# First attention one step deeper: a sequence's transposes, values and products behind the next scores, sorting counts a step later

## The reference, cut to what matters

```python
x = x + attn_a(layernorm(x), w_q, w_k, w_v1, w_v2)   # one head, width 64, causal, 512 x 512 scores per sequence
x = x + ffn(layernorm(x), Wg, W1, W2, W3)            # 8 experts, the best 2 of each token
...
queries = einsum('bse,ek->bsk', x, w_q);  keys = einsum('bse,ek->bsk', x, w_k)
attn = softmax(where(causal, queries @ keys.T * scale, -inf))
out = attn @ ((x @ w_v1) @ w_v2)
...
scores = xt @ Wg.T                                   # per token, 8 numbers
topk_scores, topk_idx = top_k(scores, 2)
```

## Time and profile before

| what | us |
|---|---|
| median of 3 runs (lowest, highest) | 1552.91 (1551.44, 1554.37) |
| the profiled execution, its own time | 1549.28 |
| its span, first to last instruction | 1547.5 |
| busy in the span: PE, DVE, ACT, POOL | 1320.2, 1109.0, 951.5, 765.4 |
| `attention_a`, first matmul (67.48) to the experts' first DMA (244.32) | 176.8 |
| start of the scores of steps 0 to 7 | 70.55, 76.81, 84.35, 92.58, 111.26, 129.12, 147.11, 165.04 |
| `slot` of b = 0 to 7 ready (start of line 742 plus 0.21) | 112.93, 130.59, 148.57, 166.50, 185.00, 199.43, 213.93, 227.01 |

### The profile page before, as it was taken

How to read it: one execution, slowest core, us unless ns; L and a number is a source line. 1 busy time by engine, 2 the same in 40 slices (tenths; PEclk the granted TensorE clock), 3 DMA queues, 4 the chain that set the end, 5 groups by cost and what they waited for, 6 DMA issues and landing times. The chain is left out here.

```text
span 1547.5 us, 28434 instructions
## 1 busy us (share of the span) xinstructions
PE 1320.2 (85%) x8377; PEld 1124.9 (73%) x8377; DVE 1109.0 (72%) x2822; ACT 951.5 (61%) x2522; POOL 765.4 (49%) x954
## 2 busy tenths in 40 slices
PE   2687635999759999999999999999999996499990
PEld 1576625888748888888888888888888884388880
DVE  5665444777638788888887888888888874377771
ACT  1554313444338878888788788787888884144440
POOL 3005562444415565576575665765755755244443
PEclk9877657999959999999999999999999996599995
DMA  9391011222100000000000000000000000122215
GB/s 182 122 364 33 30 40 48 57 57 56 31 28 15 1 15 1 1 25 5 3 25 3 17 12 1 22 8 1 11 5 5 11 1 14 39 57 56 56 44 163
DMA packets 91936, 64.47 MB, mean 42 GB/s; under 512 B 34020, under 2 KB 77935, under 8 KB 91792
## 3 DMA queue, kind: packets, MB, share of 16 engines
q1 hardware_dynamic: 83152, 45.75, 11.0%
q0 software_dynamic: 8640, 16.93, 3.5%
HBM read 26.59 MB, written 36.96 MB: 41 GB/s over the span
## 5 line engine op out<-in xcount | busy, mean ns | idle before, releaser
L1360 POOL TENSOR_TENSOR b_probs<-b_probs,b_recip 128x128 f32<-128x128 f32 (+3 forms) x512 | 352.7, 719 | 309.0 <-DVE b_recip L1593 309.0
L420 DVE TENSOR_TENSOR b_pt_lo<-b_ring,b_pt_hi 128x512 fp32r<-128x512 f32 (+1 forms) x384 | 218.9, 598 | 93.1 <-ACT b_pt_hi L414 87.8
L545 ACT ACTIVATE b_probs<-b_s_bank,b_neg_max 128x256 f32<-128x256 f32 (+3 forms) x512 | 267.9, 533 | 27.7 <-DVE b_neg_max L537 26.3
L537 DVE TENSOR_REDUCE b_neg_max<-b_s_bank 128x1 f32<-128x256 f32 (+3 forms) x512 | 219.6, 478 | 49.3 <-PE b_s_bank L529 48.3
L1220 POOL DMA_INDIRECT y_rows<-f_y_sb,f_dest x142 | 139.1, 979 | 215.4 <-DVE f_y_sb L1198 208.1
L414 ACT ACTIVATE b_pt_hi<-b_ring 128x512 fp32r<-128x512 f32 (+1 forms) x384 | 192.3, 547 | 9.1 <-PE b_ring L485 8.4
L81 PE MATMUL b_s_bank<-b_k_hi,b_q_hi 64*128 64x256 f32 (+3 forms) x512 | 181.2, 354 | 2.9 <-ACT b_probs L545 1.4
L485 PE MATMUL b_ring<-ident,b_probs 128*128 128x128 f32 x1280 | 179.4, 278 | 4.7 <-DVE b_q_lo L420 4.7
L82 PE MATMUL b_s_bank<-b_k_lo,b_q_hi 64*128 64x256 f32 (+3 forms) x512 | 164.9, 322 | 0.0
L83 PE MATMUL b_s_bank<-b_k_hi,b_q_lo 64*128 64x256 f32 (+3 forms) x512 | 164.2, 321 | 0.0
L554 PE MATMUL b_pv_bank<-b_pt_hi,b_v 128*128 128x512 f32 (+3 forms) x512 | 158.8, 322 | 6.0 <-DVE b_y L1556 4.9
(11 more groups left out here) (303 smaller groups left out, 3348.5 us busy)
## 6 DMA issues: line engine op xcount, KB each, us to landing
x_sorted<-a_blank SPq DMA_DIRECT2D x64, 260.0 KB, 3.8
f_xs<-x_sorted SPq DMA_DIRECT2D x142, 65.0 KB
b_yc<-y_rows SPq DMA_DIRECT2D x16, 256.0 KB, 3.1
f_yc<-y_rows SPq DMA_DIRECT2D x16, 256.0 KB, 3.2
y_rows<-f_y_sb,f_dest POOLq DMA_INDIRECT x142
x_tok<-in_L_attn_a_x_dram SPq DMA_DIRECT2D x8, 256.0 KB, 4.9
out_dram<-x_tok SPq DMA_DIRECT2D x8, 256.0 KB, 2.4
f_raw<-in_L_ffn_W_dram SPq DMA_DIRECT2D x1, 1408.0 KB, 6.8
```

Of the source, the lines that this page charges most:

```text
L420: nc.vector.tensor_tensor(dst, src(rg.of(key)), hi.bitcast(F32), ALU.subtract).then_inc(rg.lo_done, 1)
L537: nc.vector.tensor_reduce(sc.neg_max[:, i:i + 1], s_tile(sc, i), AX.X, ALU.max, negate=True).then_inc(sc.max_done, 1)
L545: nc.scalar.activation(probs[:, P_AT[i]:P_AT[i] + (i + 1) * P], s_tile(sc, i), ACT.Exp, bias=sc.neg_max[:, i:i + 1], accum_out=sums[:, i:i ...
L1360: nc.gpsimd.tensor_tensor(part, part, recip[:, i:i + 1].to_broadcast([P, (i + 1) * P]), ALU.mult).then_inc(probs_done, 1)
```

## The change: the later stages of a sequence move one step down

Values, transposes, and everything behind them (v hi and lo, transposed hi and lo) go from step s to step s+1, behind the next scores; products go from s-1 to s-2. `route_count` and `route_place` go from s-3 to s-4, so step 11 now has work. `output` of s-2 stays in its step but becomes PE's last item in it. The probabilities get a second buffer. The ring's order follows. On POOL, `rstd` of b+1 moves ahead of all scatters of b.

```diff
--- before.py
+++ after.py
@@ -821,11 +821,11 @@
     order = []
     for s in range(-1, NB + 4):
         order += [("q", s + 1), ("k", s + 1)] if live(s + 1) else []
+        order += [("counts", s - 4)] if live(s - 4) else []
         order += [("rows", s - 3)] if live(s - 3) else []
-        order += [("v", s)] if live(s) else []
+        order += [("v", s - 1)] if live(s - 1) else []
+        order += turns(s - 1) if live(s - 1) else []
         order += [("scores", s - 3)] if live(s - 3) else []
-        order += turns(s) if live(s) else []
-        order += [("counts", s - 3)] if live(s - 3) else []
     order += [("table", 0)]
     with ExitStack() as ctx:
         sb = lambda n, s, d: ctx.enter_context(nc.sbuf_tensor(f"a_{n}", s, d))
@@ -836,7 +836,7 @@
         rt = Route(nc, ctx, "a_r", 2, pl)
         pv_bank = pb("pv_bank")
         z_bank = pb("z_bank")
-        probs = sb("probs", [P, NPT], F32)
+        probs = [sb(f"probs{i}", [P, NPT], F32) for i in range(2)]
         pt = (sb("pt_hi", [P, NPT], F32R), sb("pt_lo", [P, NPT], F32R))
         sums = [sb(f"sums{i}", [P, QT], F32) for i in range(3)]
         recip = sb("recip", [P, QT], F32)
@@ -874,10 +874,10 @@
             rstd(nc, pool, g, rt.m, 0)
             for b in range(NB):
                 route_dest(nc, pool, g, rt, b)
+                if live(b + 1):
+                    rstd(nc, pool, g, rt.m, b + 1)
                 pool.wait_ge(blanked[b % 2], (b // 2 + 1) * NE * 16)
                 for j in range(NK * QT):
-                    if j == 2 and live(b + 1):
-                        rstd(nc, pool, g, rt.m, b + 1)
                     route_scatter(nc, pool, g, rt, b, j)
 
         @block.tensor
@@ -926,22 +926,21 @@
                     scores(s)
                 if live(s + 1):
                     project(s + 1)
-                if live(s - 1):
-                    products(s - 1)
+                if live(s - 4):
+                    route_count(nc, pe, g, rt, rg, s - 4)
+                if live(s - 2):
+                    products(s - 2)
                 if live(s - 3):
                     route_turn(nc, pe, g, rt, rg, s - 3)
+                if live(s - 1):
+                    values(s - 1)
+                    pe.wait_ge(sc.exp_done, s * QT)
+                    for k in range(len(PT_BANKS)):
+                        head_transpose(nc, pe, rg, turns(s - 1), probs[(s - 1) % 2], k, g.ident)
+                if live(s - 3):
+                    route_score(nc, pe, g, rt, rg, s - 3)
                 if live(s - 2):
                     output(s - 2)
-                if live(s):
-                    values(s)
-                if live(s - 3):
-                    route_score(nc, pe, g, rt, rg, s - 3)
-                if live(s):
-                    pe.wait_ge(sc.exp_done, s * QT + QT)
-                    for k in range(len(PT_BANKS)):
-                        head_transpose(nc, pe, rg, turns(s), probs, k, g.ident)
-                if live(s - 3):
-                    route_count(nc, pe, g, rt, rg, s - 3)
 
             for s in range(-1, NB + 4):
                 body(s)
@@ -952,27 +951,27 @@
             def body(s):
                 if live(s):
                     wait(act, recip_done, s - 2)
-                    head_exp(nc, act, sc, s, 0, probs, sums[s % 3])
-                    head_exp(nc, act, sc, s, 1, probs, sums[s % 3])
+                    head_exp(nc, act, sc, s, 0, probs[s % 2], sums[s % 3])
+                    head_exp(nc, act, sc, s, 1, probs[s % 2], sums[s % 3])
                 if live(s - 3):
                     route_apply(nc, act, g, rt, s - 3)
                 if live(s):
-                    head_exp(nc, act, sc, s, 2, probs, sums[s % 3])
+                    head_exp(nc, act, sc, s, 2, probs[s % 2], sums[s % 3])
                 if live(s + 1):
                     split_hi(nc, act, rg, ("q", s + 1), q_stack[:])
                     split_hi(nc, act, rg, ("k", s + 1), k_twice[0][:])
+                if live(s - 2):
+                    act.wait_ge(pv_full, s - 1)
+                    wait(act, z_full, s - 2)
+                    nc.scalar.activation(y_hi[:], pv_bank[:], ACT.Copy).then_inc(y_hi_done, 1)
                 if live(s - 3):
                     route_turned(nc, act, g, rt, rg, s - 3)
                 if live(s - 1):
-                    act.wait_ge(pv_full, s)
-                    wait(act, z_full, s - 1)
-                    nc.scalar.activation(y_hi[:], pv_bank[:], ACT.Copy).then_inc(y_hi_done, 1)
+                    split_hi(nc, act, rg, ("v", s - 1), v_parts[0], v_bank)
+                    for k in range(len(PT_BANKS)):
+                        head_transposed_hi(nc, act, rg, turns(s - 1), pt, k)
                 if live(s - 3):
                     route_double(nc, act, g, rt, s - 3)
-                if live(s):
-                    split_hi(nc, act, rg, ("v", s), v_parts[0], v_bank)
-                    for k in range(len(PT_BANKS)):
-                        head_transposed_hi(nc, act, rg, turns(s), pt, k)
 
             for s in range(-1, NB + 4):
                 body(s)
@@ -1002,19 +1001,18 @@
                     nc.vector.tensor_tensor(q_stack[KD:P, :], rg.of(key)[KD:P, :], q_stack[KD:P, :].bitcast(F32),
                                             ALU.subtract).then_inc(rg.lo_done, 1)
                     split_lo(nc, dve, rg, ("k", s + 1), k_twice[1][:], k_twice[0][:])
+                if live(s - 4):
+                    route_place(nc, dve, g, rt, rg, s - 4)
+                if live(s - 2):
+                    dve.wait_ge(y_hi_done, s - 1)
+                    nc.vector.tensor_tensor(y_lo[:], pv_bank[:], y_hi[:].bitcast(F32), ALU.subtract).then_inc(y_lo_done, 1)
                 if live(s - 1):
-                    dve.wait_ge(y_hi_done, s)
-                    nc.vector.tensor_tensor(y_lo[:], pv_bank[:], y_hi[:].bitcast(F32), ALU.subtract).then_inc(y_lo_done, 1)
-                if live(s):
-                    split_lo(nc, dve, rg, ("v", s), v_parts[1], v_parts[0], v_bank)
+                    split_lo(nc, dve, rg, ("v", s - 1), v_parts[1], v_parts[0], v_bank)
+                    for k in range(len(PT_BANKS)):
+                        head_transposed_lo(nc, dve, rg, turns(s - 1), pt, k)
                 if live(s - 3):
                     route_scored(nc, dve, g, rt, rg, s - 3)
                     route_rank(nc, dve, g, rt, rg, s - 3)
-                if live(s):
-                    for k in range(len(PT_BANKS)):
-                        head_transposed_lo(nc, dve, rg, turns(s), pt, k)
-                if live(s - 3):
-                    route_place(nc, dve, g, rt, rg, s - 3)
                 if live(s - 2):
                     add(s - 2)
                     moments(nc, dve, g, rt.m, s - 2, x_done, (s - 1) * QT)
```

## The result

Slower by a little: 1555.29 us median (1549.86 to 1559.49, 20 runs) against 1550.65 (1545.72 to 1554.37, 20 runs) on the same chip. The ratio is 1.0032 with an interval of 1.0021 to 1.0043. Two more measurements of the changed kernel gave 1.0025 (1.0010 to 1.0039) and 1.0026 (1.0015 to 1.0036). The prediction was 1548.9, faster by 0.26%: the sign is wrong. That the time lies in the stated range, 1541 to 1556.5, says little, since that range holds gains and losses alike.

The account below looks back on a forecast made before the run. Bound: a chain through several engines to the last scatter's end, 237.67 us. The half-clock sum gave -2.7 us, POOL's loop setting steps 4 to 6 gave -5.4; -4.0 was taken, 1552.91 to 1548.9 us, range 1541 to 1556.5.

Parts of the forecast that it names:

- the middle of the walk: Start of step 4 at 108.7 to slot of b = 5 at 201.1, with PE at half clock.
- half-clock sum: The walk with PE at half clock: last scatter ends at 235.0 against 237.67, -2.7 us.
- the gain at the end: On POOL, scatters of b = 7 follow those of b = 6 after 0.3 us, where POOL sat idle 1.88.
- Step 3's start: Steps 1 and 2 no longer wait for exp before transposes, so step 3 starts at 91.1, 1.5 us earlier.
- Step 6: Half-clock loop through PE, 18.4 us: maxima at T + 2.85, apply T + 4.9, q lo about T + 8.4.
- Steps 7 and 8: Half-clock steps without q and k: 16.5 us for step 7, 15.9 for step 8, which has no scores.
- PE's row of 9.96 at half clock: Turn, values, transposes, score and output in a row on PE: 9.96 us together at half clock.
- POOL's loop of 17.4: Apply to slot 5.1, then 0.82, eight scatters 9.85, rstd to next apply 1.66: 17.4 us.
- The ring: q stands three places ahead of rows, so the turn waits for q lo, until about T + 8.4.
- Full clock: Rival: PE at 1.00 from step 3 on, POOL's loop alone rules; -14.7 us, 1538.2. Chance 0.10.
- Landing exposed: Rival: apply waits for scatters' landing, POOL's loop 18.6 in steps 4 to 6; -0.5 us, 1552.4. Chance 0.22.
- v late: Rival: v hi about 3 us late in steps 4 to 6, on top of half clock; +6.3 us, 1559. Chance 0.13.

Follow-up runs that it names:

- after_again: The changed kernel as it is, measured again beside other runs on one chip; ratio 1.0025 to the kernel before.
- after_third: The changed kernel as it is, measured once more for comparison on another group's chip; ratio 1.0026 to the kernel before.
- lean_after: The changed kernel without the low parts of values and output, 16 matmuls a step fewer; ratio 0.9938 to the kernel before.
- counts_first: The changed kernel with counts ahead of q and k on PE and in the ring, placing ahead of q lo; ratio 0.9984, again 0.9997, to before.
- the transposes' part alone: The kernel before with only transposes, values and products a step later, output last on PE, two probability buffers; ratio 1.0022 to before.
- the repairs: On the changed kernel: counts_first, and output ahead of score with sum and moments ahead of rank (0.9994); both together 1.0012 to before.
- sum_in_gap: The kernel before with sum and moments between y lo and v lo on DVE, rstd ahead of the scatters; ratio 0.9963 to before.

## Why the prediction failed

**Bound and frame: right.** The stage moves by the end of the last scatter, and all 5 us stand there.

**The step that failed is the middle of the walk, from the start of step 4 to the slot of b = 5.** The half-clock sum had three parts. In us, with the kernel before and all three executions of the changed kernel:

| | start of step 4 | from there to slot of b = 5 | from there to the end |
|---|---|---|---|
| before | 111.26 | 88.17 | 38.24 |
| the prediction's sum | 108.7 | 92.4 | 33.9 |
| changed | 110.92 | 96.87 | 34.87 |
| after_again | 109.20 | 91.66 | 34.85 |
| after_third | 109.94 | 98.32 | 34.86 |

So the gain at the end, b = 7 right behind b = 6, was real: 3.4 us in each execution, 4.3 forecast. The early start was worth 0.3 to 2.1 us where 2.6 were forecast (the first scores of step 0 themselves differ by up to 1.5 us between these executions). The middle was put at 4.2 us over the kernel before and took 8.7 and 10.1 in two executions, 3.5 in the third. The third comes within 0.7 us of the forecast end; it took 1546.52, 2.4 us under the median of its runs. The ratios say that such executions aren't the usual ones.

For the profiled execution the end was put at 235.0 and came at 242.66. The 7.7 us, term by term:

- Step 3's start: 91.1 put, 92.94 measured, +1.8. The 1.5 us that steps 1 and 2 should gain didn't come: from the first scores of step 0 to those of step 3 are 21.92 us, before 22.03. The other 0.5 is a later start.
- Steps 3, 4, 5: +0.4, -1.3, +0.1.
- Step 6: +2.3. The turn was put at T + 8.4 in every step; it starts at T + 8.61, 9.27 and 10.17 in steps 4 to 6. In step 5 apply waits for rstd, that is for POOL (T + 5.60 instead of 4.9). In step 6 the maxima start at T + 4.43 instead of 2.85, 1.42 us behind the end of the last score row; in after_third it is T + 4.70, in after_again T + 2.87. The scores read 0.50 in steps 4 and 5 too (110.92 to 114.00 and 128.07 to 131.00), and there the maxima start at T + 2.87 and 2.86, so half clock alone isn't the cause.
- Steps 7 and 8: +1.4 and +1.0. Output is PE's last item, and its result was taken 0.1 us after T; measured is T + 1.33, 0.91 and 1.17 in steps 7 to 9, and the slot of b = 5 comes another 0.9 late for it.
- b = 6: -0.1. Handover to b = 7: +1.1; between the scatters are 1.37 us (dest 0.52 and 0.86 idle), not 0.3.

**PE's row of 9.96 at half clock: right**, 10.22 in step 6 and less where a part of it ran at 1.00 (8.54, 9.21). **POOL's loop of 17.4: right to 0.03 us**, but as a floor that binds behind a short step and that lean_after uncovers, not as the pace of every step.

**The ring.** The prediction saw the wait of turn for q lo and priced it about right: 8.4 against 8.61 in step 4. It sized the two loops at 17.4 and 18.4 against 17.97 now and let the ends of the pipeline carry the gain. That is the error of judgement: it walked one loop at a time, at one clock. The runs show steps in which the loops hand over (POOL's in step 5, PE's in step 6), so that a short step isn't kept and a long one is. counts_first shows the price of the ring's wait at the turn, with the late slot: 0.29%.

**Rivals.** Full clock: no, 0.60 to 0.74 from step 3 to 7. Landing exposed: no. The one wait named so (apply of b = 7, 8.99 us) ends at 219.99, 1.49 us after the 218.50 of the last scatter ahead of it, and 0.10 us after the end of shift. In lean_after, where shift is named, it is 1.50 us: rstd, not the landing. The caution of the Trainium skill, "Perfetto Trace Analysis", section "DMA Instruction — SWDGE (GPSIMD)", that the end of such a row isn't the landing, made no difference here: all eight had landed within 1.49 us of the last row's end. v late: by luck the sign and about the price (6.3 put, 5.1 measured), not the mechanism: in the changed kernel v hi starts 0.04 us after the values in every step. The late results stood at the scores and the output instead.

**What stays open.** Why results of PE are seen 1.5 to 5 us after their rows in some steps and not in others; why the transposes' part alone costs 0.22% when its profile shows the last scatter at 236.52 (that execution is 1.9 us under its median); why the row behind the turn runs at 1.00 in some executions and at 0.50 in others; and why the repairs don't add up. With steps of the same code between 15 and 20.6 us, single profiles can't tell.

## What to carry to other kernels

Deepening a hand-written pipeline pays only if every ring and every other engine's queue still has its slack afterwards: here the later count put q lo ahead of the turn, and the new place of rstd put all scatters of a sequence ahead of it. When two loops stand within 6% of each other (17.4 and 18.4 here), walk them together, at both clocks that the rows show, and take a forecast within 3% of the old step as "no change". Look first for idle time of the engine in series: moving the sum, its moments and rstd in the old order gave 0.37%, and the deeper order nothing.

## What the runs showed of the hardware that was not expected

The results of PE can be used only some time after the ends of its rows, and not by a constant: 0.03 to 0.04 us in most steps, 2.04, 3.12 and 3.08 for v in steps 4 to 6 of before, 3.5 to 5.1 in sum_in_gap. The late ones all stand behind rows whose granted clock reads 1.00, and the records name most of these waits "remote"; not all results behind such rows are late (0.03 us in step 6 of after_again). A row of PE is thus no proof that its work was done; the ends of matmul rows are modelled in the profile, so the rows and not the chip may be at fault. One pair of figures points that way: from the turn to v hi are 6.53 and 6.49 us in steps 5 and 6 of before, where the rows read 1.00, and 6.43 in step 7, where they read 0.50.

The clock of one and the same stretch differs between executions of one kernel: the row behind the turn in step 6 of the changed kernel read 0.50 and took 10.22 us in one, read 1.00 and took 6.40 in another. PE was busy for 9.99 of those 10.22 us and the clock stayed at 0.50 throughout.
